# One core, a four-block graph and token network: GpSimd takes the late lane's bias addition and memset first, and casts the adjacency after the late lane's masked products

## What is computed

```
# L0 gnn, three times
m = h @ weight[i];  aggr = A^T @ m;  h = gru_cell(aggr, h)
#   r, z = sigmoid(...); n = tanh(i_n + r * h_n); h = (1 - z) * n + z * h
# L2 gnn
msg_sum = a^T @ (x @ W_msg);  out = relu(x @ W_upd + msg_sum / deg + bias)
# L2 ffn, per chunk of 128 tokens and head
Y_diag = (C B^T * exp(segsum(dA))) @ (x * dt)          # masked products
Y_off  = C @ carried_state * exp(A_cum)
out = rmsnorm((Y_diag + Y_off + x * D) * silu(z)) @ W_out @ W_lin + b_lin
```

## Time and profile before

| | |
|---|---|
| median of 3 runs | 3431.71 us (3428.83 to 3431.92) |
| the profiled execution's own time | 3433.32 us |
| its span, first to last instruction | 3431.5 us |
| granted TensorE clock, mean | 0.994 |
| PE, DVE, ACT, POOL busy | 94%, 64%, 51%, 20% |
| chain that ended last | PE 56%, DVE 26%, ACT 11%, issue 5%, POOL 2% |
| one rotation | 205.8 us |

### The profile page before, as it was taken

One profiled execution on the slowest core, in us unless ns is written; L12 is line 12 of the kernel. 1 busy time (PEld: TensorE's weight loads), 2 busy tenths in 40 slices (PEclk: granted clock), 3 DMA queues, 4 the chain that ended last, 5 costly groups with the idle time before them and its releaser, 6 DMA issues.

```text
span 3431.5 us, 62674 instructions
## 1 busy us (share of the span) xinstructions
PE 3231.9 (94%) x24744; PEld 2268.1 (66%) x24776; DVE 2208.7 (64%) x7062; ACT 1752.7 (51%) x3195; POOL 693.3 (20%) x804
## 2 busy tenths in 40 slices
PE   8999999999999999999999999999999999999989
PEld 5766666666666666666666666666666666666677
DVE  3476666757567676666757567676666757566653
ACT  2237454563645537454563645537454563645524
POOL 0012122121221212122121221212122121221212
PEclk9999999999999999999999999999999999999999
DMA  3000000000000000000000000000000000000000
GB/s 132 2 7 1 20 4 17 7 1 20 4 17 7 1 22 1 19 4 17 7 1 19 4 17 7 1 22 1 19 4 17 7 1 19 1 4 4 1 8 5
DMA packets 28773, 40.68 MB, mean 12 GB/s; under 512 B 1344, under 2 KB 17728, under 8 KB 28224
## 3 DMA queue, kind: packets, MB, share of 16 engines
q1 hardware_dynamic: 28480, 36.67, 3.4%
HBM read 28.28 MB, written 4.19 MB: 9 GB/s over the span
## 4 chain that ended last, share of the span: by engine, by line
PE 56%; DVE 26%; ACT 11%; issue 5%; POOL 2%; DVEq 0%
PE ps L444 45%; ACT scratch L1068 8%; DVE scratch L1359 5%; PE ps L903 4%; DVE scratch L1362 4%; DVE scratch L1365 3%; DVE scratch L1860 3%; PE ps L453 2%; DVE x L1365 2%; PE ps L1056 2%; DVE stats L1380 2%; POOL rstd L2066 1%; ACT adjf L1068 1%; DVE xn L1362 1%; ACT xT L1068 1%
## 5 line engine op out<-in xcount | busy, mean ns | idle before, releaser
L1068 ACT ACTIVATE scratch<-scratch 128x512 f32<-128x512 f32 (+4 forms) x832 | 564.8, 691 | 278.9 <-DVE scratch L1359 128.9
L444 PE MATMUL ps<-xT,weights_sb 128*128 128x512 f32 x1152 | 560.9, 604 | 7.9 <-ACT xT L1068 7.8
L444 PE MATMUL ps<-scratch 128*128 128x128 f32 (+6 forms) x4608 | 534.4, 379 | 35.7 <-ACT adjf L1068 14.1
L2089 POOL TENSOR_SCALAR scratch<-scratch 128x512 f32<-128x512 f32 x512 | 352.6, 703 | 933.0 <-DVE scratch L1867 932.3
L1068 ACT ACTIVATE scratch<-ps 128x512 f32<-128x512 f32 (+2 forms) x512 | 286.5, 566 | 426.2 <-PE ps L444 230.7
L444 PE MATMUL ps<-weights_sb,scratch 128*128 128x128 f32 (+3 forms) x3840 | 492.6, 278 | 5.9 <-DVE scratch L1503 5.9
L444 PEld LDWEIGHTS ps<-weights_sb,scratch 128*128 128x128 f32 (+3 forms) x3840 | 442.2, 184 | 56.8 <-issue 29.2
L444 PEld LDWEIGHTS ps<-scratch 128*128 128x128 f32 (+5 forms) x4608 | 341.4, 159 | 174.2 <-issue 92.1
L903 PE MATMUL ps<-weights_sb,scratch 128*128 128x128 f32 x2048 | 307.0, 279 | 61.4 <-ACT adjf L1068 24.6
L2066 POOL TENSOR_TENSOR rstd<-ve,minus_half 128x4 f32<-128x4 f32 x126 | 142.9, 1134 | 1081.0 <-DVE ve L1362 1081.0
L1860 DVE CUSTOM_DVE_ANT_0 scratch<-ps,nomask 128x512 f32<-128x512 f32 x512 | 332.7, 683 | 10.5 <-PE ps L444 10.2
(11 more groups left out here) (166 smaller groups left out, 4520.1 us busy)
## 6 DMA issues: line engine op xcount, KB each, us to landing
adj<-adj SPq DMA_DIRECT2D x16, 1024.0 KB, 5.7
weights_sb<-weights SPq DMA_DIRECT2D x1, 4605.0 KB, 19.0
x_in<-x SPq DMA_DIRECT2D x16, 256.0 KB, 2.8
scratch<-scratch SPq DMA_DIRECT2D x32, 128.0 KB, 2.3
out<-x SPq DMA_DIRECT2D x16, 256.0 KB, 2.4
scratch<-raw SPq DMA_DIRECT2D x1, 1645.0 KB, 22.4
weights_sb<-weights SPq DMA_DIRECT2D x1, 499.0 KB, 6.5
scratch<-raw SPq DMA_DIRECT2D x1, 384.0 KB, 4.9
```

Source lines behind the costliest of these rows:

```text
L444: return pe.matmul(o, lhsT, rhs, start=start, stop=stop, **k)
L1068: return act.activation(o, a, func, **k)
L2089: pool.tensor_scalar(p, p, cut(g, G3_RI + n, 1), 1.0, ALU.mult, ALU.mult).then_inc(s["att_p"], 1)
```

## The change

In POOL's order string one "e" moves two places back: the early graph's cast is issued after the late graph's bias addition and memset. And in a rotation (`if g`) the cast also waits until the late graph's second masked product is done.

```diff
 POOL_TURNS = (
-    "llelelellllllllllllllllllellllllleleelllellllleelle"
+    "llellleellllllllllllllllllellllllleleelllellllleelle"
 )
...
 def g2_adjacency(g):
     yield
     pool.wait_ge(*done("aggr_psum", g, GNN0_STEPS - 1))
+    if g:
+        pool.wait_ge(*done("mt_ready", g - 1, 1))
     pool.tensor_copy(AF[g][:, :, :], ADJ[g][:, :, :]).then_inc(s["adjf_ready"], 1)
```

More of the change, by code:

```diff
@@ L118 @@
 POOL_TURNS = (
-    "llelellellllllllllllllllllellllllleleelllellllleelle"
+    "llellleellllllllllllllllllellllllleleelllellllleelle"
 )
```

## The result

| | before | after |
|---|---|---|
| median of 4 runs each | 3431.64 us (3428.83 to 3431.92) | 3403.04 us (3401.66 to 3404.14) |
| span of the profiled execution | 3431.5 us | 3400.6 us |
| granted TensorE clock, mean | 0.994 | 0.995 |
| chain that ended last | PE 56%, DVE 26% | PE 61%, DVE 23% |
| one rotation | 205.79 us | 203.96 us |

The ratio is 0.9918, with an interval of 0.9901 to 0.9935: faster by 0.8%, 28.6 us, of which 25.3 were forecast. Of every rotation 1.82 us is gone, where the forecast had 1.69.

The account below looks back on a forecast made before the run. DVE's order at the masked products was taken to set the pace, with PE waiting for it. Of 1.98 us freed there 1.69 was left; 15 x 1.69 = 25.3 us, giving 3406.4 us, range 3399 to 3415.

Parts of the forecast that it names:

- What bounds the kernel: At the masked products DVE's order sets the pace and PE waits; POOL's cast and addition slow products to 2.31 and 2.11.
- Addition earlier: 0: POOL's bias addition, issued after the layer norm's last row, costs nothing thanks to DVE's idle 0.79; otherwise up to 1.09.
- Memset earlier: 0: POOL's memset, following `gm_ready` beside two GRU instructions, costs 0; bound 0.73 us.
- Products 2 x 1.14: Without cast and addition beside them, DVE's two masked products let the next L1365 start 1.98 us earlier.
- Cast behind L1365: POOL's later cast waits for the L1365 behind the products, then runs beside PSUM readers; cost 0, at most 0.2 us.
- rival 1: The cast gets in front of L1365 behind the products, the 1.98 is eaten: 3432 us, chance 0.07.
- What is late next: Behind DVE's copies the L1359 waits for PE's gate matmul until 642.35, so 1.69 of 1.98 us is left.
- PE follows: PE's four gaps between 645 and 652 let it gain 1.6 us by 651.61, the remaining 0.1 soon after.
- rival 2: PE doesn't follow; only its listed gaps close, 1.33 a rotation: 20 us, 3411.7 us, chance 0.15.
- Rival 3: The gate matmul isn't the limit, so 1.98 a rotation comes back: 3402.0 us, chance 0.10.
- The sum: 15 rotations x 1.69 = 25.3 us, half-passes 0 and 16 nothing; median 3406.4 us, 0.74% less.
- Rivals 4 and 5: 4: running POOL instruction stops every DVE instruction, 3457 us, chance 0.04; 5: products stay slow without POOL, 3431.7 us, chance 0.02.

Follow-up runs that it names:

- the exchange in PE's order: Changed kernel with PE's third matmul of the carried states moved one step forward, in front of z's gate matmul: 3400.78 us, rotation 203.80 us.

## Why the prediction was right, and which step was off

*What bounds the kernel.* Right for the products: two turns of POOL's, a cast and an addition, held them 1.99 a rotation. Each was taken away alone: the addition gives 0.87, the cast 1.08.

*Addition earlier: 0.* Right, by the kernel without it. It stood for an L1365 with two SBUF inputs, as forecast.

*Memset earlier: 0.* Right, but the prediction named no reader for it. There is one, the copies; it is at ease only because the order moves too.

*Products 2 x 1.14.* Right: 2.27 from the first to the L1365 in all 15 rotations, 1.99 less than before; forecast was 1.98.

*Cast behind L1365.* Right, by a margin of 0.21; rival 1 is real, and was seen where the cast was issued earlier.

*What is late next.* This step failed. It said that the L1359 behind the copies needs the gate matmul whose other reader on ACT starts at 642.34, and cannot start before 642.35, +3.92; so 1.69 would be left. It starts at +3.62, straight behind the copies, and that ACT instruction at +3.91: the L1359 waits for `gate_psum` 4k + 2, raised by an earlier matmul than z's, which raises the next count. The small L1365 behind it wait for PE's third matmul of the carried states, which takes 0.13 back there, and 0.15 to 0.16 in the rotation. The limit was PE's order at this place, as argued, but the wrong matmul of two neighbours, and 1.82 is left. In the trace of before the L1359 starts straight behind the copies and never waits for PE, so the row couldn't show its limit; I took for it the end on PE that lies nearest, instead of counting through PE's order which of the gate matmuls it reads.

*PE follows.* Right that it does: all its waits between 645 and 652 closed, and rival 2 (1.33) is out. The size was too small: the prediction let PE gain 1.6 by 651.61 and the rest later, and it gained 1.85 by there. Of the 2.0 that it read from the gaps, 0.15 is missing there, where it had left 0.1 at each of the four to the semaphores: that allowance was too large. Rival 3, 1.98, is what the exchange in PE's order gave; in the change itself it is 0.16 too much.

*The sum.* 15 x 1.82 = 27.3 instead of 15 x 1.69 = 25.3; the fifteen intervals of the two profiles differ by 27.1. Between the medians stand 28.6, and 29.4 when it was run again; the remaining 1 to 2 us are no more than the runs of one kernel differ by (2.5 of the changed kernel, 3.1 of before). Of the 3.4 between 3406.4 forecast and 3403.04 measured, 2.0 are the mis-sized step; for the rest no cause is shown.

*Rivals 4 and 5.* Out: nothing that reads PSUM was slower beside the cast, nor was the L1359 at 600.55 beside the addition (0.69), and the products became short. But the prediction's "with at most one SBUF input DVE is left alone" was read from rows with inputs in PSUM and is too wide: the mask has one input, in SBUF, and POOL's power stood for it all the same.

## What to carry to other kernels

Read an engine's instruction whose duration is longer than the same form's elsewhere as a wait that the profile doesn't name, and look which instruction of the other engine began just before it; here two such meetings a rotation cost 0.8% of the kernel, and a third, a mask beside a small power on the chain, another 0.3% (3392.54 us; 15 times 0.92 would be 13.8 us, the medians show about 10). Move the reading instruction of the engine that has time so that it is issued after, not before, the last one on the chain that wants two SBUF inputs; behind that it may run freely. Before a wait is added, move away what is queued behind it: the same wait without the reordering made the kernel 0.7% slower.

## What the runs showed of the hardware

- In every meeting read here the turn went by the start of the instruction as the profile has it, and a lead of 0.09 us was enough: the addition at 633.18 against the product at 633.27 made that product take 2.11. With the cast issued after the first product, the standing cast was served before DVE's next instruction, which was queued right behind the running one (L1365 at 2.38).
- A DVE tensor_scalar from int32 to float over 128x2048 with one SBUF input makes POOL's power take 1.91 instead of 1.01; so it is not two inputs alone that lock. The Trainium skill ("SBUF — State Buffer", SBUF: two separate sides) names instructions in a mode that uses two ports as a second such class; the trace names no mode. It does show that this one passes 2048 columns in 1.22, where a product takes 1.22 for 1024; that speaks for such a mode and doesn't prove it. The copies from PSUM and the L1359 with a PSUM input stayed at 0.72 and 0.69 beside the cast.
- A memset of 1.80 on POOL beside a two-input product left it at 1.21.
- The first 220 us, in which the edits change next to nothing, differ by up to 7.7 us between profiled executions, with a granted clock between 0.94 and 0.98 there (by 2.1 between two executions of the very same kernel), while a rotation repeats to 0.03 within an execution and to 0.01 between those two. The difference of two spans has to be cut at the first repetition before it is laid to an edit. What decides how much clock is granted there stays open.
